# A routed stage two slots later and seven attention halves of nine slots, in a feed-forward / attention / feed-forward layer on one core

## The chip, the cores and the metric

The kernel runs on one core of one Trainium2 chip. The metric is the device time of one execution in microseconds (us); lower is better. TensorE is called PE below, VectorE DVE, ScalarE ACT, GpSimd POOL and SyncE SP, as in the profile.

## What is computed

The input `x` is four images of 512 x 512 f32 (2048 rows of 512). Three sublayers follow each other, each on a layer norm of its input:

```python
x = x + 0.5 * _L0_ffn_ref(_layernorm(x), w12, w3, router_w, expert_bias, sw1, sw2, sw3)
x = x + _L0_attn_ref(_layernorm(x), qkv_w, conv..., proj..., ln...)
x = x + 0.5 * _L0_ffn_ref(_layernorm(x), ...)          # the same weights again
```

`_L0_ffn_ref` adds a shared part, `silu(x @ sw1.T) * (x @ sw2.T) @ sw3.T` with 2048 hidden units, and a routed part: each row picks 2 of 8 experts (256 hidden units each) by a sigmoid router, and the experts' results are added with normalised weights. `_L0_attn_ref` is attention in windows of 8 tokens of 16 channels, with a three-tap convolution of the values, a projection and a norm.

## The kernel before, in words

**Slots.** The order of the work is written out by hand in slots, and all engines walk through the same slots. There are `SLOTS_ALL` = 128, in eight units of `UNIT` = 16: units 0 to 3 are the four images of the first feed-forward sublayer, units 4 to 7 those of the second. A slot `s` is 128 hidden units of the shared part for one image. PE does in it the gate product (12 matmuls, L1484), the up product (12, L1484), and the down product of the slot before it (12, L1498) into four PSUM banks. ACT makes the silu of the gate (L1694), DVE multiplies it with the up product (`sgh`, L1854), ACT takes the high bf16 half (L1704) and POOL the low half (L1812). The gate product of slot s+1 waits for the silu of s, the up product of s+1 for DVE's `sgh` of s, and the down product of s for POOL's low half. So DVE or ACT work that is late in a slot reaches PE in the next.

**Between the products** PE does small pieces into two side banks, listed with a slot and a position 0 to 5 in `PIECES` (L978 and on): the transposes and router logits of a row tile (`third`, `logits`; L463, L481), the transposes and products of attention (`turn` L1103, `qkv` L1120, `back`, `proj`, `out` L1301), and the lists of the routing (L749). ACT copies each piece out of its bank, in the order of its program, at the same position.

**Routed stages.** `ROUTED_AT` (L86) names the two slots ahead of which a routed stage of NB = 39 blocks stands, (23, 116): PE's L1607, L1620, L1632, rows gathered by POOL (L1801), results stored by SP in `sorted_y` (L1448). In the slots after it a class `Combine` adds the experts' results to the rows: `COMBINE_SLOT` (L1024 to 1026) gives tile m its slot. POOL gathers its two sets of rows from `sorted_y` (L665) and SP loads the row itself (L671, from `x2p`) one slot ahead; DVE adds (L686, L689); SP stores (L677). Three tiles are in flight: a buffer is free when the tile three before it has been stored. Tiles 28 to 31, the last image's, are not stored but stay in SBUF; tile 31's gather and load wait until tile 29 has been added. After slot 127 the down product of slot 127 is done, DVE adds the PSUM banks to tiles 28 to 31 (L578, `Evac(LAST).vec_sum`), and SP stores the output (L605).

**Evacuations.** `EVACS` (L523) gives ten slots (`EV_AT`) in which DVE adds an image's shared sum to rows that SP has loaded in slot `EV_LOAD` (L530 to 532). One of them stands at each routed stage (`EV_AT[1]`, `EV_AT[8]`), and the last at slot 128.

**Attention** is done for half an image at a time (8 halves), beside the slots. `D_SLOT` (L943) is where half h starts on DVE, `B_SLOT` where it ends (the next half's start). Slots `D_SLOT - 2` and `D_SLOT - 1` hold its `turn` and `qkv` pieces. DVE's 21 tasks of a half (products L1147, sums L1153, maxima, merging) are spread over the slots from `D_SLOT` to `B_SLOT` by `spare` and `WORK_SLOT`, a planner with fixed costs for each slot's other DVE work. `EXP_SLOT` is the slot after a maximum: ACT does the exponential there (L1203), at the end of its slot, with a table load before it and another before the next silu. `NORM_SLOT` is `B_SLOT + 2` (norm of the half, square root on ACT L1282), and `OUT_AT` two slots later. For image i the row tiles of the second feed-forward sublayer (`TILE`) begin when its second half is out, and the last image's tiles lead to the router, the lists (`LIST_SLOT`), and the gathers of the routed stage (`GATHER_SLOT`).

The slots of before:

| | before |
|---|---|
| `ROUTED_AT` | 23, 116 |
| `D_SLOT` | 29, 38, 47, 55, 64, 73, 81, 90 (the last half ends at 99) |
| slots of each half | 9, 9, 8, 9, 9, 8, 9, 9 |
| second `EXP_SLOT` of each half | 34, 43, 52, 61, 69, 78, 86, 95 |
| `turn` pieces of halves 1 to 7 | 36, 45, 53, 62, 71, 79, 88 |
| `LIST_SLOT[1]`, `GATHER_SLOT[1]` | 111, 114 |
| combine tiles 27 to 31 | 123, 124, 124, 125, 126 |
| shared weights reloaded (ACT queue; gate and up L304, 1 MB; down L311, 0.5 MB) | L304 in odd slots, the last in 123; L311 two slots after each |

Of the kernel before, what the change touches and what calls it, by code (L numbers as in the profile page):

```python
# [58 lines left out]
def macaron(nc, x, wall, rwT, ebias, qkvw, projw, projb, convw, convb, lnw, lnb, out):  # L59
# [7 lines left out]
    NT = ROWS // P  # L67
# [9 lines left out]
    HALVES = 2 * IMAGES  # L77
# [5 lines left out]
    UNIT = NU * KT  # L83
    UNITS = 2 * IMAGES
    SLOTS_ALL = UNITS * UNIT
    ROUTED_AT = (UNIT + 7, 7 * UNIT + 4)  # L86
    assert W3OFF + KT * D == WW and NB == 39 and UNIT == 16 and NU == E and NT == 16


# [12 lines left out]
    with ctx:  # L102
# [415 lines left out]
        def pool_root(e, q, var, root, n):  # L518
# [4 lines left out]

        EVACS = [(UNIT, 0, x, x1p, False), (ROUTED_AT[0], 1, x, x1p, False), (2 * UNIT, 1, x1p, x1d, True),
                 (3 * UNIT, 2, x1p, x1d, True), (4 * UNIT, 3, x1p, x1d, True), (5 * UNIT, 0, x2d, x2p, False),
                 (6 * UNIT, 1, x2d, x2p, False), (7 * UNIT, 2, x2d, x2p, False), (ROUTED_AT[1], 3, x2d, x2p, False),
                 (8 * UNIT, 3, None, out, False)]
        EV_AT = [ev[0] for ev in EVACS]
        EV_STORED = [16 * (v + 1 + sum(ev[4] for ev in EVACS[:v + 1])) for v in range(len(EVACS))]
        EV_LOAD = [at - 5 for at in EV_AT]  # L530
        EV_LOAD[0], EV_LOAD[1], EV_LOAD[2], EV_LOAD[3], EV_LOAD[4], EV_LOAD[5], EV_LOAD[6], EV_LOAD[8] = (
            UNIT - 2, EV_AT[1] - 4, EV_AT[2] - 2, EV_AT[3] - 3, EV_AT[4] - 4, EV_AT[5] - 3, EV_AT[6] - 2, EV_AT[8] - 1)
        LAST = len(EVACS) - 1

        class Evac:
# [404 lines left out]
        BIAS_SLOT, BIAS_STEPS = UNIT - 4, (4, 4, 4, 3)  # L940
        CONST_SLOT = 1
        LOADED, STATS, NORMED, HIGH, LOW, TURNED, LOGITS = range(7)
        D_SLOT = [ROUTED_AT[0] + 6 + 9 * h - h // 3 for h in range(HALVES)]  # L943
        LOAD_SLOT = [ROUTED_AT[0] + 1, ROUTED_AT[0] + 5] + [d - 4 for d in D_SLOT[2:]]
        B_SLOT = D_SLOT[1:] + [D_SLOT[-1] + 9]
        NORM_SLOT = [b + 2 for b in B_SLOT[:-1]] + [B_SLOT[-1] + 2]
# [28 lines left out]
        GATHER_SLOT = [s + 3 for s in LIST_SLOT]  # L975
        assert all(GATHER_SLOT[f] < ROUTED_AT[f] for f in range(2))

# [5 lines left out]
        for h in range(HALVES):  # L983
            d, b, end = D_SLOT[h], B_SLOT[h], h == HALVES - 1
            PIECES += [(d - 2, m, "turn", h, m) for m in range(2)]
# [29 lines left out]
        def spare(h, s):  # L1015

            left = 7.5 - 0.8 + sum(PE_SHARE.get(p[2], 1.0) for p in PIECES if p[0] == s)
            left -= sum(2.2 * (t[STATS] == s) + 0.6 * (t[NORMED] == s) + 0.7 * (t[HIGH] == s) + 0.7 * (t[LOW] == s) for t in TILE)
            left -= 7.0 * (s in NORM_SLOT) + 2.8 * (s in EV_AT)
            left -= sum(2.1 * (0 <= s - at - 1 < 2) + 0.3 * (0 <= s - at - 2 < 2) for at, ev in zip(EV_AT, EVACS) if ev[4])  # L1020
            left -= sum((1.5 + 2.0 * (m < TI)) * (at == s) for m, at in enumerate(COMBINE_SLOT))
            return max(left, 0.5)

        COMBINE_SLOT = [ROUTED_AT[0] + 1 + 2 * (m // 3) + m % 3 // 2 for m in range(8)]  # L1024
        COMBINE_SLOT += [2 * UNIT + 5 + m for m in range(8)]
        COMBINE_SLOT += [ROUTED_AT[1] + 2 * (m // 3) + m % 3 // 2 for m in range(NT)]
        WORK_SLOT = []
        for h, (d, b) in enumerate(zip(D_SLOT, B_SLOT)):
            left = [spare(h, s) for s in range(d, b)]
# [994 lines left out]
```

## Time and profile before

| | |
|---|---|
| three timed runs | 1465.43, 1465.55, 1476.45 us; median 1465.55 |
| the profiled execution | 1469.57 us |
| its span, first to last instruction | 1467.8 us |
| mean granted PE clock | 0.998 of full speed |
| PE busy | 1417.9 us, 97% |
| DVE, ACT, POOL busy | 952.1, 551.7, 502.1 us |

The span is what the rows below are times of, in us from its start; 1.77 us of the profiled execution lie around it. PE is busy nearly always, so what can be won or lost is in the places where it is not.

### The profile page before, as it was taken

The numbers are of one execution on the slowest core, as the hardware profiler recorded it, in microseconds if no ns is written. First come the engines' busy times: TensorE is split into PE (matmuls) and PEld (weight loads), VectorE is DVE, ScalarE is ACT, GpSimd is POOL, SyncE is SP. The second block draws the span as 40 slices with busy tenths as digits, with TensorE's granted clock in tenths as the row PEclk, the third lists the DMA queues.
The fourth block names the chain that finished last, engine by engine and source line by source line (L and its number), as shares of the span: only waits on it lengthen the run. The fifth ranks groups of instructions, "written<-read, shape, count | busy, mean of one in ns | idle before, by whom it ended". The sixth has DMA issues, their size and how long they took to land.

```text
span 1467.8 us, 22015 instructions
## 1 busy us (share of the span) xinstructions
PE 1417.9 (97%) x7642; PEld 679.6 (46%) x7642; DVE 952.1 (65%) x1295; ACT 551.7 (38%) x1153; POOL 502.1 (34%) x424
## 2 busy tenths in 40 slices
PE   4999999999989999999999999999999999999998
PEld 2444444444444444444444544445454444444443
DVE  5778853333348798998889889988935643333343
ACT  4566323333232433354544454345332213333211
POOL 2321132221244556263436343443512122221343
PEclk9999999999999999999999999999999999999999
DMA  9999668888493467174616562365327368898595
GB/s 305 306 351 320 267 143 206 194 196 183 165 279 119 153 189 235 44 215 132 185 52 181 168 144 83 112 188 143 109 87 227 103 183 219 188 195 185 189 300 185
DMA packets 233725, 272.63 MB, mean 186 GB/s; under 512 B 132243, under 2 KB 156819, under 8 KB 230163
## 3 DMA queue, kind: packets, MB, share of 16 engines
q1 hardware_dynamic: 198594, 166.34, 39.5%
q10 hardware_dynamic: 23664, 67.66, 14.7%
q0 software_dynamic: 11360, 37.23, 9.4%
q8 instruction: 66, 1.08, 0.3%
q14 instruction: 41, 0.33, 0.1%
HBM read 168.39 MB, written 72.88 MB: 164 GB/s over the span
## 4 chain that ended last, share of the span: by engine, by line
PE 62%; DVE 13%; issue 7%; DMA 3%; ACT 2%; POOL 2%; SPq 0%; POOLq 0%; ACTq 0%; DVEq 0%
PE bank L1484 25%; PE bank L1607 13%; PE bank L1498 12%; PE bank L1632 7%; DVE region L1147 3%; PE side L1120 1%; DVE region L1153 1%; DMA rows<-sorted_y,slots 1%; DVE sgh L1854 1%; PE side L1620 1%; POOL rows L665 1%; DVE rows L455 1%; PE side L1253 1%; DVE rows L446 1%; DMA region<-region 1%
## 5 line engine op out<-in xcount | busy, mean ns | idle before, releaser
L1484 PE MATMUL bank<-xT,wb 128*128 128x512 bf16 x2688 | 615.7, 381 | 23.6 <-DMA xT<-region 17.7
L1484 PEld LDWEIGHTS bank<-xT,wb 128*128 128x128 bf16 x2688 | 257.7, 98 | 324.9 <-issue 29.7
L1812 POOL TENSOR_TENSOR hs<-sgh,hs 128x512 bf16<-128x512 f32 x126 | 161.1, 1278 | 626.6 <-ACT hs L1704 626.5
L1498 PE MATMUL bank<-wb,hs 128*128 128x512 bf16 x1536 | 357.1, 379 | 0.2 <-POOL hs L1812 0.2
L1498 PEld LDWEIGHTS bank<-wb,hs 128*128 128x128 bf16 x1536 | 147.6, 98 | 173.3 <-issue 2.1
L1607 PE MATMUL bank<-wr,region 128*128 x912 | 221.7, 379 | 0.0
L1704 ACT ACTIVATE hs<-sgh 128x512 bf16<-128x512 f32 x128 | 81.4, 636 | 338.9 <-DVE sgh L1854 328.5
L1147 DVE TENSOR_TENSOR region<-region 128x1024 f32<-128x1024 f32 x128 | 186.9, 1482 | 1.1
L1854 DVE TENSOR_TENSOR sgh<-bank,sgh 128x512 f32<-128x512 f32 x128 | 88.0, 687 | 145.1 <-PE bank L1484 144.8
L1801 POOL DMA_INDIRECT region<-xnd,idxs x78 | 74.2, 952 | 221.3 <-DMA region<-region 214.0
L1694 ACT ACTIVATE sgh<-bank 128x512 f32<-128x512 f32 x128 | 76.6, 598 | 189.4 <-PE bank L1484 183.6
L1153 DVE TENSOR_REDUCE region<-region 128x256 f32<-128x2048 f32 x64 | 146.3, 2286 | 2.2
L1607 PEld LDWEIGHTS bank<-wr,region 128*128 128x128 bf16 x912 | 85.9, 98 | 89.9 <-issue 1.0
L1632 PE MATMUL bank<-wr,region 128*128 x468 | 113.7, 379 | 0.0
L1951 DVE TENSOR_TENSOR region<-bank,region 128x256 f32<-128x256 f32 x76 | 32.3, 425 | 97.8 <-ACT region L1742 91.3
L665 POOL DMA_INDIRECT rows<-sorted_y,slots x64 | 67.1, 1049 | 79.1 <-issue 73.7
L1742 ACT ACTIVATE region<-bank 128x256 f32<-128x256 f32 x76 | 29.2, 384 | 172.3 <-PE bank L1607 167.8
L1961 DVE COPY region<-side 128x512 bf16<-128x512 bf16 x78 | 33.1, 425 | 83.5 <-PE side L1620 83.5
L1484 PE MATMUL bank<-region,wb 128*128 128x512 bf16 x384 | 85.9, 379 | 1.5 <-DVE sgh L1854 1.5
L686 DVE SCALAR_TENSOR_TENSOR rows<-rows,coef 128x512 f32<-128x512 f32 x32 | 28.2, 880 | 71.6 <-DMA rows<-x2p 22.1
L1632 PEld LDWEIGHTS bank<-wr,region 128*128 128x128 bf16 x468 | 45.8, 98 | 55.2
L1484 PEld LDWEIGHTS bank<-region,wb 128*128 128x128 bf16 x384 | 37.4, 98 | 46.9 <-DVE sgh L1854 2.0
(182 smaller groups left out, 1356.0 us busy)
## 6 DMA issues: line engine op xcount, KB each, us to landing
wb<-wsplit ACTq DMA_DIRECT2D x42, 1024.0 KB
wb<-wsplit ACTq DMA_DIRECT2D x42, 512.0 KB
sorted_y<-region SPq DMA_DIRECT2D x78, 256.0 KB
wsplit<-wb SPq DMA_DIRECT2D x8, 1536.0 KB, 7.6
wr<-wall SPq DMA_DIRECT2D x6, 1536.0 KB, 9.8
rows<-x SPq DMA_DIRECT2D x32, 256.0 KB, 5.3
region<-xln SPq DMA_DIRECT2D x128, 64.0 KB, 2.6
xnd<-rows SPq DMA_DIRECT2D x30, 256.0 KB, 4.5
```

The lines of the kernel that those rows point to most:

```text
L665: e.indirect_dma_start(out=dst, out_offset=None, in_=sorted_y, in_offset=bass.IndirectOffsetOnAxis(ap=slots[:, self.f, k, self.t:self.t + ...
L1147: o.do(e.tensor_tensor(t, few.to_broadcast(full), many.to_broadcast(full), ALU.mult))
L1153: o.do(e.tensor_reduce(dst[:, (k - 1) * P:(k + 1) * P], self.tmp.rearrange("p (n c) -> p n c", c=H), AX.X, ALU.add))
L1484: m = e.matmul(ps[:], wb[:, w % 2, wp, at:at + P], xt[:, xp, c, :], start=(i == 0), stop=(i == 3 * NDC - 1))
L1498: m = e.matmul(psD[tt][:], hs[:, s % 2, hp, tt * P:(tt + 1) * P], wb[:, w % 2, wp, at:at + D], start=(first and i == 0), stop=(last and i ...
L1607: m = e.matmul(psH_of(k)[:], xsT[k % RX][:, xp * D + c * P:xp * D + (c + 1) * P], words_of(k, wp, c * D), start=(n == 0), stop=(n == 3 * N ...
L1632: m = e.matmul(psY[k % 2][:], hT[k % 2][:, hp, kt, :], words_of(k, wp, at), start=(n == 0), stop=(n == 3 * KT - 1))
L1694: e.activation(sgh[:, s % 2, :], psG[:], ACT.Silu).then_inc(S("h_silu").sem, 1)
L1704: e.activation(hs[:, s % 2, 0, :], sgh[:, s % 2, :], ACT.Copy).then_inc(S("h_hi").sem, 1)
L1801: e.indirect_dma_start(out=xs[k % RX], out_offset=None, in_=xnd, in_offset=bass.IndirectOffsetOnAxis(ap=idxs[:, k:k + 1], axis=0)).then_in ...
L1812: e.tensor_tensor(hs[:, s % 2, 1, :], sgh[:, s % 2, :], hs[:, s % 2, 0, :], ALU.subtract).then_inc(S("h_lo").sem, 1)
L1854: e.tensor_tensor(sgh[:, s % 2, :], psU[:], sgh[:, s % 2, :], ALU.mult).then_inc(S("h_mul").sem, 1)
```

## The change

The second routed stage stands ahead of slot 118 instead of 116 (its combine tiles move with it, and the last of them are held at slot 127), and the attention halves start one slot later from half 3 on, except half 5. Three loads of evacuations start one or two slots later.

```diff
-    ROUTED_AT = (UNIT + 7, 7 * UNIT + 4)
+    ROUTED_AT = (UNIT + 7, 7 * UNIT + 6)
...
         EV_LOAD = [at - 5 for at in EV_AT]
-        EV_LOAD[0], EV_LOAD[1], EV_LOAD[2], EV_LOAD[3], EV_LOAD[4], EV_LOAD[5], EV_LOAD[6], EV_LOAD[8] = (
-            UNIT - 2, EV_AT[1] - 4, EV_AT[2] - 2, EV_AT[3] - 3, EV_AT[4] - 4, EV_AT[5] - 3, EV_AT[6] - 2, EV_AT[8] - 1)
+        EV_LOAD[0], EV_LOAD[1], EV_LOAD[2], EV_LOAD[3], EV_LOAD[4], EV_LOAD[5], EV_LOAD[6], EV_LOAD[7], EV_LOAD[8] = (
+            UNIT - 2, EV_AT[1] - 4, EV_AT[2] - 2, EV_AT[3] - 3, EV_AT[4] - 4, EV_AT[5] - 2, EV_AT[6] - 1, EV_AT[7] - 3,
+            EV_AT[8] - 1)
...
-        D_SLOT = [ROUTED_AT[0] + 6 + 9 * h - h // 3 for h in range(HALVES)]
+        D_SLOT = [ROUTED_AT[0] + 6 + 9 * h - (h > 4) for h in range(HALVES)]
...
-        COMBINE_SLOT += [ROUTED_AT[1] + 2 * (m // 3) + m % 3 // 2 for m in range(NT)]
+        COMBINE_SLOT += [min(ROUTED_AT[1] + 2 * (m // 3) + m % 3 // 2, SLOTS_ALL - 1) for m in range(NT)]
```

What these give, worked out from the formulas:

| | after |
|---|---|
| `ROUTED_AT` | 23, 118 |
| `D_SLOT` | 29, 38, 47, 56, 65, 73, 82, 91 (the last half ends at 100) |
| slots of each half | 9, 9, 9, 9, 8, 9, 9, 9 |
| second `EXP_SLOT` of each half | 34, 43, 52, 61, 70, 79, 87, 96 |
| `turn` pieces of halves 1 to 7 | 36, 45, 54, 63, 71, 80, 89 |
| `LIST_SLOT[1]`, `GATHER_SLOT[1]` | 112, 115 |
| combine tiles 27 to 31 | 125, 126, 126, 127, 127 |
| `EV_LOAD` of the evacuations at 80, 96, 112 | 78, 95, 109 (before: 77, 94, 107) |

## Rows read from the trace of the kernel before

**Rows 1.** The page: busy time of the engines.
```profile
PE 1417.9 (97%) x7642; PEld 679.6 (46%) x7642; DVE 952.1 (65%) x1295; ACT 551.7 (38%) x1153; POOL 502.1 (34%) x424
```

**Rows 2.** Timeline of PE, slots 51 to 95: start, length, instruction, [idle before it, releaser].
```profile
631.36 1.47 PE L1484 MATMUL bank<-xT,wb 128*128 128x512 bf16 x6 [1.62 <-ACT sgh L1694]
...
698.55 0.20 PE L481 MATMUL side<-rw,xT 128*128 128x24 bf16 x2 [0.72 <-ACT rows L472]
...
737.15 0.92 PE L1120 MATMUL side<-wqkv,region 64*128 64x192 f32 x8 [1.12 <-ACT region L1112]
...
861.00 0.20 PE L481 MATMUL side<-rw,xT 128*128 128x24 bf16 x2 [0.33 <-ACT rows L472]
...
870.89 0.66 PE L1301 MATMUL side<-ident,region 128*128 128x128 f32 x4 [0.46 <-ACT region L1306]
...
893.67 0.92 PE L1120 MATMUL side<-wqkv,region 64*128 64x192 f32 x8 [2.60 <-ACT region L1112]
...
1026.39 0.66 PE L1301 MATMUL side<-ident,region 128*128 128x128 f32 x4 [0.18 <-ACT region L1306]
```

**Rows 3.** Timeline of PE, the later places where it sat idle over 0.5 us.
```profile
1136.80 0.38 PE L463 MATMUL side<-identb,rows 128*128 128x128 bf16 x4 [1.48 <-DVE rows L455]
...
1188.52 0.75 PE L749 MATMUL side<-rows 128*128 128x78 bf16 x16 [0.60 <-DVE rows L743]
...
1386.05 2.76 PE L1484 MATMUL bank<-region,wb 128*128 128x512 bf16 x12 [1.48 <-DVE sgh L1854]
```

**Rows 4.** Timeline of ACT at the end of slot 78: half 5's second exponential.
```profile
888.81 1.28 ACT L1203 ACT_TABLE_LOAD   x1
890.11 0.63 ACT L1203 ACTIVATE region<-region 128x512 f32<-128x512 f32 x1
...
891.24 1.28 ACT L1694 ACT_TABLE_LOAD   x1
```

**Rows 5.** Timeline of PE and DVE at the end of slot 48's up product.
```profile
611.43 2.76 PE L1498 MATMUL bank<-wb,hs 128*128 128x512 bf16 x12
...
612.07 0.68 DVE L1854 TENSOR_TENSOR sgh<-bank,sgh 128x512 f32<-128x512 f32 x1
```

**Rows 6.** Busy times by stretch, slots 27 and 28; granted clock after the five engines.
```profile
413.00:421.00 8.00, 6.23 (x19) 3.35 (x20) 3.35 (x7) 1.79 (x3) 2.51 (x3) 0.57 0.79 239
```

**Rows 7.** Timeline of PE, slots 126 and 127: the down products that follow the up product.
```profile
1450.81 2.75 PE L1498 MATMUL bank<-wb,hs 128*128 128x512 bf16 x12
...
1458.58 2.75 PE L1498 MATMUL bank<-wb,hs 128*128 128x512 bf16 x12
```

**Rows 8.** Timeline of SP, its queue: the loads of the combine tiles 27 and 28 on.
```profile
1430.19 0.47 SPq L671 DMA_DIRECT2D rows<-x2p  x1
...
1439.32 6.88 SPq L671 DMA_DIRECT2D rows<-x2p  x4
```

**Rows 9.** Timeline of DVE, slots 123 to the end: combine tiles 27, 28, 31, and the last sums.
```profile
1437.38 0.75 DVE L686 SCALAR_TENSOR_TENSOR rows<-rows,coef 128x512 f32<-128x512 f32 x1 [6.99 <-DMA rows<-x2p]
...
1442.83 0.75 DVE L686 SCALAR_TENSOR_TENSOR rows<-rows,coef 128x512 f32<-128x512 f32 x1 [3.31 <-DMA rows<-x2p]
...
1445.78 0.68 DVE L1854 TENSOR_TENSOR sgh<-bank,sgh 128x512 f32<-128x512 f32 x1
...
1453.57 0.75 DVE L686 SCALAR_TENSOR_TENSOR rows<-rows,coef 128x512 f32<-128x512 f32 x1 [1.79 <-DMA rows<-sorted_y,slots]
...
1462.43 2.63 DVE L578 SCALAR_TENSOR_TENSOR rows<-bank,rows 128x512 f32<-128x512 f32 x4 [2.89 <-PE bank L1498]
```

**Rows 10.** Timeline of POOL: tile 31's second gather, and slot 127's low half.
```profile
1450.04 0.95 POOL L665 DMA_INDIRECT rows<-sorted_y,slots  x1 [0.31 <-issue]
...
1460.28 1.15 POOL L1812 TENSOR_TENSOR hs<-sgh,hs 128x512 bf16<-128x512 f32 x1 [6.61 <-ACT hs L1704]
```

**Rows 11.** Timeline of ACT: a reload of shared weights (its queue), and slot 127's high half.
```profile
1430.43 0.53 ACTq L304 DMA_DIRECT2D wb<-wsplit  x1
...
1459.58 0.63 ACT L1704 ACTIVATE hs<-sgh 128x512 bf16<-128x512 f32 x1 [2.73 <-DVE sgh L1854]
```

## The prediction

> **What bounds the kernel now.** I read the page first, then the list of PE's waits, then PE's timeline for every idle place, and last the timelines of DVE, ACT, POOL and SP around those places. PE is busy 1417.9 us of 1467.8 [rows 1]; no other engine is above 65%. So the time is PE's work, which the change leaves alone (the same products, pieces and blocks in another order), and about 50 us in which PE sits idle. Of these, some 39 us lie before slot 51 or behind the last product and are not moved by the change of slots; in the reach of the change are seven places in the attention stretch, 1.62 + 0.72 + 1.12 + 0.33 + 0.46 + 2.60 + 0.18 = 7.03 us [rows 2], and three later ones, 1.48 + 0.60 + 1.48 = 3.56 us [rows 3]. If all ten went, the gain would be 10.6 us, 0.7%. That is the ceiling, and it is below 1% (14.7 us), which is about what a measurement of this kernel can tell from no change.
>
> **The routed stage two slots later.** It removes and adds no instruction. Its 39 blocks follow each other on PE without a gap in the trace, and a gap of 1.48 us comes behind it, where DVE waited in the stage's first slot for the first gathered rows and was then late for the up product (the row at 1386.05) [rows 3]. The tiles, their gathers and loads, and the even and odd slots of the weight reload move by two together, so this gap moves along: 0, bounded by its whole loss (-1.48) and by as much again (+1.48). Ahead of the stage the gathers get a slot more of slack; nothing waited there, so that is worth 0. The last image's tiles, routing and lists come one slot later. The 1.48 at L463 (DVE busy with two tiles in one slot) moves with them. The 0.60 at L749 stays too: DVE has one list and the evacuation together in slot 112, before and after; only it is now the first list. 0 for both, with bounds of -2.1 and +1.5 (one more such wait).
>
> **The end.** Here the change costs. Tile 31's place would be slot 128 and is cut to 127, and tiles 28 to 31 now stand in slots 126, 126, 127, 127. I call U the end of the last up product, 1458.58, and a slot without pieces is 1458.58 - 1450.81 = 7.77 us [rows 7]. Everything of tiles 27 to 30 comes two slots (15.54 us) later against U: what stood at a time t of the trace stands at t - 1443.04 from U.
> - Tile 27's load was issued at 1430.19 and used at 1437.38, 7.2 us later; a reload of shared weights, 1 MB, was issued beside it at 1430.43 [rows 8, 9, 11]. The last reload from an odd slot leaves at 123, so in its new place, slot 124 to 125, none is beside it. Tile 28's load, which had none either, took 1442.83 - 1439.32 = 3.5 us [rows 8, 9]. I take 3.5 us: issued at U - 12.85, used at -9.35, two DVE additions of 0.79 us each: done at -7.75.
> - Then SP stores 27 and loads 28 and 29, at -7.4; used at -3.9; both tiles take 1445.78 - 1442.83 = 2.95 us [rows 9]: done at -0.95, so DVE's `sgh` of slot 127 is not held up.
> - Tile 31's two gathers wait for that. POOL does them in its slot 126, ahead of the low half of slot 127: 0.95 + 0.30 + 0.95 = 2.2 us [rows 10], until +1.25. The low half can only start when the high half is there, 1460.21 - 1458.58 = +1.63 [rows 10, 11]; so the last down product is not delayed.
> - The rows land 1453.57 - 1450.99 = 2.6 us after the gather's issue ends [rows 9, 10], at +3.85. Tile 31's row load, issued at about -0.95, is there by +2.6. Meanwhile DVE does `sgh` and tile 30. Tile 31: two additions, 1.6 us, to +5.4. The four last sums, 2.63 us [rows 9], to +8.1. Before they ended at 1465.06 - 1458.58 = +6.5.
> So the end is 1.6 us later. Bounds: if the gathers land before DVE asks for them, DVE has `sgh`, then tiles 30 and 31 (3.2 us) behind it: 0.95 + 3.2 + 2.63 = +6.8, or 0.3 later. If tile 27's load takes 7.2 us in its new place too, all of it is 3.7 us later: the gathers stand until +4.95, the low half until +6.1 (before +2.85, 1460.28 + 1.15), so PE waits 3.25 us, and the last sum ends at +11.8: 5.3 later. I take 1.6, since the loads in question are nearest to the row without a reload beside them.
>
> **The halves.** The exponential of a half ends its ACT slot; with two table loads it keeps ACT for 1.28 + 0.63 + 1.28 us, and the copy of the next half's `turn` piece stands behind the first two of these [rows 4]. This costs PE where the second exponential is in the slot right before the `turn`: before, at slots 52/53, 61/62, 78/79. PE waited 0, 1.12 and 2.60 us for it [rows 2]. After, there are two such pairs, 70/71 and 79/80. Half 4 (8 slots from 65) has the planner's task list of half 2 before it (8 slots from 47) to within a task: 0. Half 5 (9 slots from 73) has that of half 3 before it (9 slots from 55) to within a task: 1.12. So 3.72 becomes 1.12: 2.60 gained.
> The 1.62 us in slot 51 come from a late silu: in slot 49 to 50 DVE was late with the norm of half 1 and ACT's root behind it. Half 2 had four products and two sums in slot 47; now it has three products and one sum, and slot 48 costs the same as before. DVE was 612.07 - 611.43 = 0.64 us late at the end of slot 48 [rows 5], and that lateness goes: 0.6 gained, 1.0 stays. The other four (1.69 us together) are copies of tiles' and halves' pieces that are short of time by under a microsecond; their slots shift against each other and I let them stand at 0 change. Sum of the halves: -3.2 us, with bounds of -7.0 (all gone) and +1.0: if both new pairs cost what the worst old one did, 5.2 us stand for 3.72 (+1.5), less the 0.6. Where such a wait goes, DVE's `sgh` of that slot is late next; PE needs it only after a down and a gate product, 2 x 2.59 us, so a lateness like the 2 to 3 us that goes with it stays hidden.
> One rule of the Trainium skill would make this larger: "ScalarE: Activation LUTs", section "What ACT_TABLE_LOAD costs", says that a switch of tables costs the load and a drain of 1380 ns behind it, 2.66 us in all. By this each pair would hold ACT for over 5 us and the pair removed would be worth about twice as much. The trace shows no drain: the load from 888.81 takes 1.28 us and the exponential begins 0.02 us behind it [rows 4].
>
> **The loads of evacuations.** Those of slots 80, 96 and 112 are issued one or two slots later, for they wait for tiles that come later. The tightest is that of 96, issued in slot 95 behind the piece at position 4. Four loads take under 7.2 us to land in the worst row for such a load [rows 8, 9], and their sums must be done when the down product of slot 96 begins, a whole slot after its up product; at 7.77 us a slot they fit, by about 1 us in that worst case. Worth 0; if the cover were gone, 1 to 2 us.
>
> **Sum.** -3.2 + 1.6 + 0 = -1.6 us. The profiled execution was 1469.57 us (1467.8 and 1.77 around), so a profile of after would be 1468.0. The median of the runs is 4.02 us below the profiled execution; a part may be that in slots 27 and 28 the granted clock was 0.57 over 8 us [rows 6], which is 3.4 us lost to the lower of the two levels, 1.2 GHz, after PE had sat idle for a load. Nothing before slot 47 is changed, so I leave this difference as it is: 1465.55 - 1.6 = 1464.0 us.
>
> **Rivals.**
> - **A: the combine queue runs into slot 127 (slower).** Tile 27's load does not get faster, tile 31's gathers hold POOL ahead of the last low half, PE waits and the last sums come late: +5.3, with the halves' -3.2 it is +2.1, 1467.7 us; up to 1470.8 if the halves give nothing. It decides from where the load takes 1.6 us longer than 3.5, that is 5.1 us, for then the end costs the 3.2 that the halves give. For it: DVE waited 6.99 and 3.31 us for such loads [rows 9]. Against it: the reload beside it is gone. Chance 0.25.
> - **B: nine slots are enough everywhere.** All seven waits of rows 2 go: -7.0 + 1.6 = -5.4, 1460.1 us. For it: all come from late ACT or DVE. Against it: two exponentials still stand right before a `turn`. Chance 0.15.
> - **C: the waits only move.** The shifted slots meet evacuations and tiles in new ways, and the halves give 0: +1.6, 1467.2 us. For it: six of the seven waits are under 1.7 us, each a chance meeting. Chance 0.18.
> - **D: the clock.** PE sits idle in a new place and is granted 1.2 GHz for a while: 3.4 us for each stretch as in rows 6. Four or more would be needed to pass 1%. Chance 0.04, here for slower by over 1%.
> - **The forecast**, 0.38, with an own range of 1462 to 1466.
>
> **The range.** The low end is case B with half a microsecond less, 1459.5; the high end case A with the halves giving almost nothing, 1470.5. Faster by over 1% lies beyond the ceiling of 10.6 us and would need something that I don't see: 0.01. Slower by over 1%: case D, 0.04. Within 1%: 0.95.
>
> **What would show it.** Right: in PE's timeline of the two waits for L1112 (1.12 and 2.60 us) one is left, of about 1 us, in slot 80, and there is none in slots 54, 63 and 71; the wait of 1.62 us in slot 51 is near 1.0; the routed stage is followed by a wait of about 1.5 us; tile 27's row is used 3 to 4 us after its load; DVE's last four sums end about 8 us after the last up product. Wrong: a PE wait for POOL (L1812) of several us before the last down product (case A); no waits over 0.5 us between slots 51 and 104 (case B); several new ones there that add to 7 us (case C); a clock under 0.99 in the mean (case D).

## The result and the profile after

The changed kernel is slower: 1473.4 us median (1471.16 to 1476.34, 5 runs) against 1465.82 us (1465.43 to 1476.45, 5 runs); the ratio of the runs is 1.0039, 95% interval 1.0021 to 1.0057, that is +5.7 us (+3.1 to +8.4). The profiled execution of after is 1472.36 us, with a span of 1470.6. The forecast was 1464.0 with a range up to 1470.5; the outcome lies beyond it, on rival A's side.

The two profiles differ by only 2.8 us in their spans, because they differ already where nothing was changed. DVE's product of slot 46, the last slot before half 2's new plan, starts at 594.37 us before and at 589.98 after (some waits were shorter, and PE ran at the lower clock for 3.4 us there, from 83.3 us on, instead of the 6.8 us of [rows 6]). So I count from there. The busy times by stretch have the lengths: slots 46 to 99 (the halves), 99 to 115, 115 to the end of the last up product (routed stage, combine tiles), and from there to the last instruction. Before:

```profile
594.37:1069.12 474.75, 467.23 (x2604) 230.05 (x2603) 431.36 (x435) 214.09 (x495) 206.28 (x139) 1.00 0.47 136
1069.12:1203.62 134.50, 132.42 (x728) 63.42 (x727) 65.23 (x141) 36.94 (x65) 27.20 (x24) 1.00 0.47 144
1203.62:1458.58 254.96, 253.48 (x1291) 119.25 (x1289) 85.68 (x166) 69.12 (x141) 78.17 (x79) 1.00 0.79 216
1458.58:1467.80 9.22, 5.51 (x25) 2.17 (x23) 3.32 (x5) 0.63 (x1) 1.15 (x1) 1.00 0.31 114
```

After (stretch, its length, busy PE, weight load, DVE, ACT, POOL; granted clock):

```profile
589.98:1062.97 472.99, 464.10 (x2560) 230.77 (x2611) 424.84 (x430) 215.71 (x496) 203.32 (x139) 1.00 0.47 137
1062.97:1197.77 134.80, 131.72 (x713) 63.28 (x727) 70.71 (x146) 37.05 (x65) 27.73 (x24) 1.00 0.43 132
1197.77:1455.29 257.52, 253.79 (x1266) 119.75 (x1289) 78.32 (x159) 69.13 (x141) 76.74 (x77) 0.99 0.83 215
1455.29:1470.60 15.31, 7.10 (x24) 2.53 (x23) 8.79 (x13) 0.63 (x1) 3.45 (x3) 0.84 0.40 137
```

The halves gave 1.76 us, slots 99 to 115 took 0.3, the third stretch 2.56, the end 6.09: together +7.2 us, in the timed interval. The places, in PE's timeline after:

```profile
627.94 1.47 PE L1485 MATMUL bank<-xT,wb 128*128 128x512 bf16 x6 [2.32 <-ACT sgh L1695]
...
807.22 0.63 PE L1104 MATMUL side<-ident,region 128*128 128x128 f32 x4 [1.00 <-DMA region<-xln]
...
895.29 0.92 PE L1121 MATMUL side<-wqkv,region 64*128 64x192 f32 x8 [1.11 <-ACT region L1113]
...
1182.08 0.75 PE L750 MATMUL side<-rows 128*128 128x78 bf16 x16 [0.60 <-DVE rows L744]
...
1396.61 4.45 PE L1485 MATMUL bank<-region,wb 128*128 128x512 bf16 x12 [2.41 <-DVE sgh L1855]
...
1462.34 4.40 PE L1499 MATMUL bank<-wb,hs 128*128 128x512 bf16 x11 [4.30 <-POOL hs L1813]
```

Of the seven waits of [rows 2] the two for the `turn` copy have become one of 1.11 us, as forecast; the one in slot 51 has grown from 1.62 to 2.32; one of 1.00 for a half's load is new. The 1.48 behind the routed stage is 2.41, and before the last down product stands a wait of 4.30 us for POOL, which was 0.16 before. After both long waits PE runs its matmuls at the lower of its two clock levels (1.2 GHz) for a while; in the first line the four microseconds after the wait, in the second those after the 4.30 us:

```profile
1397.00:1401.00 4.00, 4.00 (x13) 1.47 (x11) 0.96 (x2) 0.81 (x2) 3.25 (x3) 0.57 0.86 256
1462.00:1466.00 4.00, 3.61 (x9) 1.33 (x11) 2.20 (x4) 0.00 (x0) 0.28 (x1) 0.57 0.18 56
```

At 0.57 over 4 us, 1.7 us of full speed are lost to PE each time. The first loss is in the third stretch: 0.93 us more wait and these 1.7 us make its 2.56. The second costs the kernel nothing in this profile. DVE begins the last sums when tile 31 is added (1465.22) and does the four without a pause, so PE, slow or not, is ahead of them. The five runs of after have mean clocks of 0.994 to 0.997. The profile of before has 0.998, but before's runs beside e5 to e12 go from 0.994 to 1.000, so these means alone tell little.

The end itself is in DVE's, POOL's and SP's timelines after. DVE:

```profile
1447.00 0.75 DVE L687 SCALAR_TENSOR_TENSOR rows<-rows,coef 128x512 f32<-128x512 f32 x1 [5.13 <-DMA rows<-x2p]
...
1455.25 0.75 DVE L687 SCALAR_TENSOR_TENSOR rows<-rows,coef 128x512 f32<-128x512 f32 x1 [6.11 <-DMA rows<-x2p]
...
1458.15 0.68 DVE L1855 TENSOR_TENSOR sgh<-bank,sgh 128x512 f32<-128x512 f32 x1
...
1463.77 0.75 DVE L687 SCALAR_TENSOR_TENSOR rows<-rows,coef 128x512 f32<-128x512 f32 x1 [3.48 <-DMA rows<-sorted_y,slots]
1464.56 0.75 DVE L690 SCALAR_TENSOR_TENSOR rows<-rows,coef 128x512 f32<-128x512 f32 x1
1465.22 2.48 DVE L579 SCALAR_TENSOR_TENSOR rows<-bank,rows 128x512 f32<-128x512 f32 x4
```

The row loads in the timeline of SP's queue, after:

```profile
1441.67 0.49 SPq L672 DMA_DIRECT2D rows<-x2p  x1
...
1448.94 9.64 SPq L672 DMA_DIRECT2D rows<-x2p  x4
```

POOL's timeline of after:

```profile
1448.15 1.21 POOL L666 DMA_INDIRECT rows<-sorted_y,slots  x1 [0.30 <-issue]
...
1458.51 0.95 POOL L666 DMA_INDIRECT rows<-sorted_y,slots  x1 [4.77 <-DVE rows L690]
1459.76 1.34 POOL L666 DMA_INDIRECT rows<-sorted_y,slots  x1 [0.30 <-issue]
1461.12 1.16 POOL L1813 TENSOR_TENSOR hs<-sgh,hs 128x512 bf16<-128x512 f32 x1
```

Tile 27's row was used 5.3 us after its load (1441.67 to 1447.00), tile 28's 6.3 us after (1448.94 to 1455.25), where I had 3.5 for both. In the first of them nearly all was moved after 3.3 us; the busy times by stretch show the DMA engines almost still behind that, at 8 GB/s (the last number; before it their busy share):

```profile
1441.67:1445.00 3.33, 3.33 (x17) 1.54 (x16) 0.20 (x1) 0.63 (x1) 1.76 (x2) 1.00 0.85 300
1445.00:1446.00 1.00, 1.00 (x6) 0.42 (x5) 0.00 (x0) 0.60 (x1) 0.69 (x2) 1.00 0.05 8
```

Tiles 28 and 29 then hold DVE's product of slot 127 until 1458.15, 2.9 us behind the up product (1455.29); tile 31's gathers wait for tile 29's sum and stand ahead of the low half of slot 127, which ends at 1462.3. The last sums end 12.4 us behind the last up product, against 6.5 before.

### The profile page after: what moved, and what is told of

The parts are those of the page before. It is cut to its first block, busy times and chain, and to the rows that moved or that the text cites. A ratio compares the mean times of both kernels' runs of the same rounds, so it can differ in the third digit from the quotient of the medians.

```text
span 1470.6 us, 21867 instructions
## 1 busy us (share of the span) xinstructions
PE 1410.4 (96%) x7493; PEld 679.7 (46%) x7642; DVE 946.5 (64%) x1295; ACT 553.7 (38%) x1154; POOL 499.2 (34%) x424
## 4 chain that ended last, share of the span: by engine, by line
PE 62%; DVE 10%; issue 6%; DMA 6%; ACT 2%; SPq 1%; POOL 1%; POOLq 0%; DVEq 0%; ACTq 0%
PE bank L1485 24%; PE bank L1608 13%; PE bank L1499 12%; PE bank L1633 7%; DMA rows<-x2p 2%; DMA rows<-sorted_y,slots 2%; PE side L1121 2%; DVE region L1148 1%; PE side L1621 1%; DMA region<-xln 1%; DVE rows L687 1%; DVE rows L690 1%; PE side L1254 1%; POOL rows L666 1%; DVE sgh L1855 1%
## 5 line engine op out<-in xcount | busy, mean ns | idle before, releaser
L1485 PE MATMUL bank<-xT,wb 128*128 128x512 bf16 x2613 | 605.7, 381 | 27.3 <-DMA xT<-region 17.8
L1608 PE MATMUL bank<-wr,region 128*128 x889 | 216.8, 379 | 1.2
L1633 PE MATMUL bank<-wr,region 128*128 x458 | 111.6, 379 | 0.5
L687 DVE SCALAR_TENSOR_TENSOR rows<-rows,coef 128x512 f32<-128x512 f32 x32 | 25.1, 784 | 73.6 <-DMA rows<-x2p 31.1
```

The lines of the kernel that those rows point to most:

```text
L1485: m = e.matmul(ps[:], wb[:, w % 2, wp, at:at + P], xt[:, xp, c, :], start=(i == 0), stop=(i == 3 * NDC - 1))
L1608: m = e.matmul(psH_of(k)[:], xsT[k % RX][:, xp * D + c * P:xp * D + (c + 1) * P], words_of(k, wp, c * D), start=(n == 0), stop=(n == 3 * N ...
L1633: m = e.matmul(psY[k % 2][:], hT[k % 2][:, hp, kt, :], words_of(k, wp, at), start=(n == 0), stop=(n == 3 * KT - 1))
```

## Experiments

Each kernel was timed against the kernel before on the same chip. "End" is from the last up product to the last instruction, "halves" from slot 46 to 99, each in that kernel's profile (before: 9.2 and 474.75 us). Waits are PE's, in us. Ratios of after, of e1 to e4, of e5 to e8, of e9 to e11 and of e12 come from five separate comparisons, and the profile is one execution of each.

| | ratio to before, 95% | halves | wait in slot 51 | behind the routed stage | PE's wait for POOL at the end | end |
|---|---|---|---|---|---|---|
| before | 1 | 474.75 | 1.62 | 1.48 | 0.16 | 9.2 |
| after | 1.0039 (1.0021-1.0057) | 472.99 | 2.32 | 2.41 | 4.30 | 15.3 |
| e1 | 1.0048 (1.0030-1.0067) | 474.81 | 2.32 | 1.87 | under 0.3 | 9.2 |
| e2 | 1.0038 (1.0023-1.0052) | 474.55 | 1.62 | 1.73 | 3.02 | 13.7 |
| e3 | 1.0016 (1.0003-1.0028) | 474.31 | 2.32 | 1.76 | 2.11 | 13.2 |
| e4 | 1.0046 (1.0033-1.0059) | 472.68 | 2.32 | 1.43 | 2.56 | 17.3 |
| e5 | 1.0004 (0.9993-1.0015) | 474.86 | 2.32 | 2.04 | 2.15 | 13.4 |
| e6 | 1.0023 (1.0011-1.0035) | 472.62 | 2.32 | 3.20 | 1.72 | 12.7 |
| e7 | 1.0010 (0.9996-1.0024) | 474.05 | 2.33 | none | 1.31 | 12.1 |
| e8 | 0.9999 (0.9979-1.0019) | 474.70 | 1.62 | none | under 0.3 | 9.5 |
| e9 | 0.9999 (0.9985-1.0013) | 473.28 | 2.32 | 1.56 | 0.72 | 10.7 |
| e10 | 0.9997 (0.9980-1.0014) | 476.49 | 2.31 | 0.68 | 0.72 | 10.0 |
| e11 | 0.9981 (0.9967-0.9994) | 472.78 | 1.50 | none | 1.50 | 11.8 |
| e12 | 0.9996 (0.9979-1.0013) | 473.66 | 1.46 | 1.74 | 1.50 | 11.9 |

**e1: the halves alone.** 
```diff
-    ROUTED_AT = (UNIT + 7, 7 * UNIT + 6)
+    ROUTED_AT = (UNIT + 7, 7 * UNIT + 4)
```


> The change without its first part: the second routed stage stays ahead of slot 116, the attention halves and evacuation loads are those of after. Theory 'the end' (the loss is made by combine tiles 28 to 31 in slots 126 and 127: late product on DVE, POOL's low half behind tile 31's gathers, PE idle before the last down product): the loss is gone, 1 to 4 us faster than before (1462 to 1465), and DVE's last sums end about 6.5 us behind the last up product as before. Theory 'the halves' (their new slots cost in the timed runs, by waits or by a lower clock after them): still 3 to 8 us slower than before.

The end is that of before (9.2 us), but the kernel is 7.0 us slower, where 1 to 4 us faster was expected if only the end made the loss. PE's waits in this profile show what the later halves do when the routed stage does not move:

```profile
1205.22 2.76 PE L1608 MATMUL side<-wr,region 128*128 x12 [1.67 <-DMA region<-region]
...
1212.50 1.47 PE L1608 MATMUL bank<-wr,region 128*128 x6 [1.93 <-DMA region<-region]
```

The gathers for the stage are issued in slot 115, one slot ahead of it, and its first blocks wait 1.67 + 1.93 = 3.6 us for their rows. With 118 no first block waits (in e4 a later one does once, 1.06 us): the two slots of delay pay for the halves' slot. From slot 46 on this profile takes 5.0 us more than before's, of which these are 3.6. And the gain of the halves is lost to the clock: the wait in slot 51 is 2.32 us as in after, and here the clock falls behind it (granted clock 0.57 in the column before the last two), where in after it did not:

```profile
626.00:630.00 4.00, 1.68 (x9) 0.60 (x8) 3.93 (x4) 3.37 (x4) 2.60 (x2) 1.00 0.00 0
630.00:634.00 4.00, 4.00 (x15) 2.01 (x14) 3.83 (x11) 3.13 (x4) 2.83 (x3) 0.57 0.34 130
```

That brings the halves' stretch back to 474.8 us. In the nine profiles with a wait of about 2.3 us there, the length of this stretch falls in two groups: 472.6 to 473.3 (after, e4, e6, e9), and 474.0 and more (e1, e3, e5, e7, e10): the second group are those with the lower clock behind the wait. So the 1.8 us that the halves give are lost again in five of these nine executions.

**e2: the routed stage alone.** 
```diff
-        D_SLOT = [ROUTED_AT[0] + 6 + 9 * h - (h > 4) for h in range(HALVES)]
+        D_SLOT = [ROUTED_AT[0] + 6 + 9 * h - h // 3 for h in range(HALVES)]
```
(and `EV_LOAD` as before)

> The first part alone: routed stage ahead of slot 118 with its combine tiles, halves and loads as before. Theory 'the end': the whole loss and none of the small gain, 6 to 9 us slower than before; PE idle about 4 us for POOL before the last down product, last sums ending about 12 us behind the last up product. Theory 'the halves': within 2 us of before.

5.6 us slower (3.4 to 7.6), a little less than the 6 to 9 expected; the end is 4.5 us longer than before's (6.1 in after) and PE waits 3.02 us for POOL. The last sums end 10.8 us behind the up product (1457.81 to 1468.64). The first part of the change makes the end long with no help from the halves.

**e3: tile 31 on buffers of its own.** 
```diff
                 if m == 2 * NT - 1:
-                    self.r = T(6)
+                    self.a, self.b, self.r = (words(R_QKV + k * D, D) for k in range(3))
...
-                    e.wait_ge(S("c_sum").sem, 2 * NT - 2)
+                    return
```


> After, with three buffers of its own for combine tile 31 (in the region that the routed stage has left free) and semaphores of its own, so that its gathers and its load wait for no other tile. Theory 'the end': POOL is free for slot 127's low half, so PE's wait of 4.3 us shrinks to the 2 to 3 us by which DVE's product of slot 127 is late; last sums end 8 to 10 us behind the last up product; 2 to 4 us faster than after, about as before or up to 3 slower. If POOL's wait had no part in it: as after.

As expected: PE's wait falls to 2.11 us and the end by 2.1 us. The ratio is 1.0016 where it was 1.0039; the two intervals overlap. By the profile the wait of tile 31's gathers for tile 29 costs some 2 us.

**e4: tile 31's gathers behind the low half.** 
```diff
-                        if c.m % NT >= WAYS:
+                        if c.m % NT >= WAYS and c.m < 2 * NT - 1:
                             c.pool_gather(e)
+                    if s == SLOTS_ALL - 1:
+                        Combine(2 * NT - 1).pool_gather(e)
```


> After, with tile 31's two gathers behind the low half of slot 127 in POOL's order instead of ahead of it. Theory 'the end' in two parts: PE's wait before the last down product falls from 4.3 to about 3 us (what DVE's late product leaves), but the gathers start 2 us later, so tile 31's sum and with it the end come 1 to 3 us later than in after. If only POOL's order made the loss: 2 to 4 us faster than after.

PE's wait falls to 2.56 us, which is what DVE's late product leaves, and the end is 2.0 us longer than in after, as tile 31's sum starts at 1467.94, 10.5 us behind the up product. Both parts count: POOL's order for PE, the gathers' landing for the last sums. Swapping them only moves the loss; the timed runs (1.0046 against 1.0039) can't tell the two kernels apart.

**e5: own buffers for tiles 28 to 31, rows loaded early.** 
```diff
-                if m == 2 * NT - 1:
-                    self.r = T(6)
+                if m >= KEPT:
+                    self.a, self.b, self.r = (words(R_QKV + (3 * (m - KEPT) + k) * D, D) for k in range(3))
...
+                    if 4 <= s - ROUTED_AT[1] < 4 + TI:
+                        Combine(KEPT + s - ROUTED_AT[1] - 4).sp_load(e)
```


> After, with three buffers of their own for each of combine tiles 28 to 31 (twelve, in the region the routed stage has left free), their row loads issued in slots 122 to 125 ahead of SP's stores, and no waits for other tiles. Theory 'the end is a chain of buffers' (store, load, add, gather): the chain is cut, PE's wait for POOL before the last down product is under 0.5 us, the last sums end about 6.5 to 7.5 us behind the last up product instead of 12.4, and the kernel is 4 to 6 us faster than after, so within 2 us of before. Rival 'the DMA engines are full' (about 290 GB/s in the last slots whatever waits): the gathers still land late, PE waits 2 us or more, and it is at most 2 us faster than after.

The time came as expected (5 us below after, level with before), the profile only in part: PE still waits 2.15 us for POOL. POOL's timeline says why:

```profile
1454.24 1.15 POOL L1821 TENSOR_TENSOR hs<-sgh,hs 128x512 bf16<-128x512 f32 x1 [0.52 <-ACT hs L1713]
1455.54 1.24 POOL L668 DMA_INDIRECT region<-sorted_y,slots  x1
1457.08 1.39 POOL L668 DMA_INDIRECT region<-sorted_y,slots  x1 [0.30 <-issue]
1458.78 0.95 POOL L668 DMA_INDIRECT region<-sorted_y,slots  x1 [0.30 <-issue]
1460.03 0.95 POOL L668 DMA_INDIRECT region<-sorted_y,slots  x1 [0.30 <-issue]
1460.99 1.16 POOL L1821 TENSOR_TENSOR hs<-sgh,hs 128x512 bf16<-128x512 f32 x1
```

Nothing is waited for, but the four gathers of tiles 30 and 31 take 5.4 us of POOL between the low halves of slots 126 and 127, and they start late because tile 27's row (4.65 us of wait) made slot 126 late.

**e6: only the rows' loads early.** e5 with the gathers' buffers and waits as in after.

> As e5, but only the rows' own loads (from x2p) of tiles 28 to 31 have buffers of their own and leave early; the gathers stay where they are, and tile 31's still waits for tile 29's sum. If the row load behind the store is what makes DVE late at slot 127 (5.3 and 6.3 us of wait in after), DVE's product of slot 127 comes within 1 us of the last up product's end and PE's wait for POOL falls below 1.5 us: 3 to 5 us faster than after. If the gathers are as late as the loads, DVE waits for them instead, and the gain is under 2 us.

DVE's product of slot 127 now starts 0.6 us behind the up product (1460.77 and 1460.15), so the row loads behind the stores were what made it late; PE's wait is 1.72 us (under 1.5 was expected) and the end 12.7 us. The gain on after is 2.3 us by the ratios, less than the 3 to 5 expected; in this profile 3.20 us were lost behind the routed stage, with the clock at the lower level after it.

**e7: stage at 117, combine tiles one slot behind it, with the buffers of e5.** 
```diff
-    ROUTED_AT = (UNIT + 7, 7 * UNIT + 6)
+    ROUTED_AT = (UNIT + 7, 7 * UNIT + 5)
...
-        COMBINE_SLOT += [min(ROUTED_AT[1] + 2 * (m // 3) + m % 3 // 2, SLOTS_ALL - 1) for m in range(NT)]
+        COMBINE_SLOT += [min(ROUTED_AT[1] + 1 + 2 * (m // 3) + m % 3 // 2, SLOTS_ALL - 1) for m in range(NT)]
```


> The halves of after, the routed stage ahead of slot 117, the first combine tiles one slot behind it (118) instead of in its first slot, the last at 127, and the own buffers of e5. Expected: the first block is not waited for (a slot of slack, against 1.7 and 1.9 us in e1), no wait for DVE behind the routed stage (1.5 to 2.4 us before), the end as in e5; about 3 us faster than before in the stretches, less what the lower clock takes. If the wait behind the routed stage comes from something else than the combine tiles in its first slot, it stays.

The wait behind the stage is gone, so it does come from the combine tiles in its first slot. A new one of 2.59 us stands in the stage's first blocks, after DVE's evacuation had waited for its rows (L579, 1.09 and 1.05 us, from x2d); it is there again in e10 (2.69) and e11 (1.27, after 3.43 for a block's rows), all three with the stage ahead of an odd slot, and in none with 116 or 118. I read it as the evacuation's loads meeting the weight reload of the odd slot before; that was not tested. The 3 us of gain that were expected did not come: from slot 46 on this profile takes 5.3 us more than before's, and the timed runs are level with before.

**e8: before, with the later combine tiles and own buffers.** The same two edits on the kernel before.

> Before (old halves, routed stage ahead of 116) with its combine tiles one slot later (117 to 127) and the own buffers of e5. Expected: the 1.48 us wait behind the routed stage is gone, the end is no longer than before (9.2 us from the last up product to the last instruction): 1 to 3 us faster than before. If a tile in slot 127 costs by itself, whatever its buffers: 2 us or more slower.

The profile does what was expected (no wait, end 9.5 us, 1.4 us shorter from slot 46 on), and a tile in slot 127 costs nothing by itself. The 1 to 3 us of gain expected are not seen in the timed runs (1463.69 to 1479.26), which can't tell it from before.

**e9: e5 with the gathers spread.** 
```diff
+                    early = {SLOTS_ALL - 4: [KEPT], SLOTS_ALL - 3: [KEPT + 1, KEPT + 2], SLOTS_ALL - 2: [KEPT + 3]}
-                    for c in combines(s + 1):
+                    for c in [c for c in combines(s + 1) if c.m < KEPT] + [Combine(m) for m in early.get(s, [])]:
```


> e5 (own buffers for tiles 28 to 31) with POOL's eight gathers of them spread: tile 28 in slot 124, 29 and 30 in slot 125, 31 alone in slot 126, where e5 has two tiles in each of 125 and 126. Theory 'four gathers of 1.25 us each stand ahead of slot 127's low half': PE's wait for POOL, 2.15 us in e5, falls below 0.6 us and the end from the last up product on is about 10 to 11 us instead of 13.4: 1 to 3 us faster than e5, as fast as before or 1 to 2 us faster. If the wait is DVE's late product instead, it stays at 2.

POOL's timeline of e9:

```profile
1455.96 1.24 POOL L668 DMA_INDIRECT region<-sorted_y,slots  x1
1457.50 0.95 POOL L668 DMA_INDIRECT region<-sorted_y,slots  x1 [0.30 <-issue]
1458.88 1.71 POOL L1821 TENSOR_TENSOR hs<-sgh,hs 128x512 bf16<-128x512 f32 x1 [0.43 <-ACT hs L1713]
```

With two gathers ahead of it the low half waits for ACT again, PE waits 0.72 us (under 0.6 was expected), and the end is 10.7 us. In the profile this takes from slot 46 on 873.6 us, against 873.4 before and 880.6 after. In the timed runs it is level with before, and 0.5 thousandths from e5, less than can be told.

**e10 and e11: e7 with the gathers spread, and with half 2 at eight slots.** 
```diff
-        D_SLOT = [ROUTED_AT[0] + 6 + 9 * h - (h > 4) for h in range(HALVES)]
+        D_SLOT = [ROUTED_AT[0] + 6 + 9 * h - (h > 4 or h == 3) for h in range(HALVES)]
```
(the second edit, e11 only)

> e7 (halves of after, routed stage ahead of 117, first combine tiles one slot behind it, own buffers) with the gathers spread as in e9. Expected: no wait behind the routed stage, PE's wait for POOL at the end (1.3 us in e7) under 0.6 us, and 1 to 3 us faster than before in the timed runs if the 2.59 us wait inside the routed stage of e7 was a single event; if it comes back, 0 to 2 us slower.

> e10 with half 2 back at eight slots (47 to 54) and half 3 from 55 with ten. Theory 'half 2's ninth slot takes DVE work out of slot 47, which had time for it, and leaves slot 48 as full as it was': the wait of 2.32 us in slot 51 is 1.62 us again as in before, and no stretch of lower clock follows it. Rival: the wait comes from the norm of half 1 alone: it stays at 2.3.

e10 is level with before, its odd-slot wait back, and two of the waits expected to be small or absent are 0.68 us (behind the stage) and 0.72 us (for POOL). e11 has 1.50 us in slot 51, so half 2's ninth slot made the longer wait; no lower clock follows there, nor in e12 (1.46), before, e2 and e8 (1.62). e11 is the only kernel whose interval lies below 1 (0.9967 to 0.9994), by 2.8 us. Its profile doesn't show that gain: from slot 46 on it takes 881.0 us, as long as after's 880.6 and 7.5 us more than before's. Its span is short (1467.2 us) because slot 46 begins at 586.22 us, 8.2 us earlier than in before, and in the slots up to there the two kernels do the same. The timed gain goes with the clock: means of 0.997 to 0.999 in all twelve runs, 0.994 to 0.999 in before's 29. Why the clock was higher is not known.

**e12: e9 with half 2 at eight slots.**

> e9 (routed stage ahead of 118 as in after, own buffers, gathers spread) with half 2 at eight slots as in e11. Expected: the wait in slot 51 at 1.5 to 1.6 us instead of 2.32, PE's wait for POOL at the end under 1 us, no wait inside the routed stage (those of e7, e10 and e11 came with its odd slot 117), one of about 1.5 us behind it: 1 to 3 us faster than before in the timed runs, as e11. If e11 owes its time to the combine tiles' later first slot, this one is no faster than before.

The waits are as expected but for POOL's (1.50, where under 1 was expected), and the time is level with before (0.9979 to 1.0013), not 1 to 3 us faster. So e11's gain is not confirmed by its nearest relative, and of twelve comparisons one just beyond its interval is thin; I would call e11 no slower than before in the timed runs; a gain that comes from the changed slots is not shown.

## Why the prediction was wrong, step by step

- **What bounds the kernel**: held. PE's work is unchanged, and all differences are waits and the clock behind them. The ceiling of 10.6 us for a gain was not approached by any version. That the later loads of the evacuations cost nothing held too: in after PE waits nowhere over 0.3 us between slot 80 and the 1.49 us at L463.
- **The end**: this step failed. I took tile 27's and 28's row loads at 3.5 us because no weight reload is issued beside them, from one row of before [rows 8, 9]. They measured 5.3 and 6.3, so DVE's last product was late where I had it on time. The load of tile 28 is the larger part: it left 1.1 us later than I had it, took 2.8 us more, and together that is 3.9 us. In before, the tile 28 row that I copied had the gathers of tiles 28 and 29 ahead of it (tile 27 had been so late that they had been issued, 1432.95 to 1437.67, before the load at 1439.32 left); a 0.5 MB reload, which I had overlooked, was issued at 1440.73, but only 0.06 MB of it had moved when the row was used. In after the gathers are issued up to 1449.36 and the load leaves at 1448.94, in the middle of them. While DVE waited for it, the gathers' queue moved 0.78 MB in after and 0.19 MB in before; in e2, e3 and e4 it was 0.36 to 0.55 MB and the same load took 4.2 to 4.4 us. In all, 287 GB/s were moved in after and 295 in before, so the engines were as full both times; the queue of the row's load had 44% of their time in after and 67% in before. No weights were moved beside it in after. I read it so: what was beside the load was replaced, not removed; no run takes the gathers alone away.
  Tile 27's 5.3 us are another matter. The gathers of tiles 28 and 29 begin to move only at 1446.0, and the engines were almost still for a microsecond before that. The last of the queue's packets come one behind the other, as from one of the 16 engines, until 1446.5. In the same window one packet of 16 KB of another queue (q8, instruction) takes 0.95 us from 1444.42 on; such a packet lies in this load's window in e2, e3 and e4 too, where it took 5.5 to 5.9 us. Whether it holds the last packets up was not tested, so the cause of tile 27's time stays open.
  From there the chain ran as the step had it, and close to the figures of rival A: DVE 2.9 us late (A: 2.7), PE idle for POOL 4.30 (A: 3.25), last sums at +12.4 (A: +11.8), the end 6.1 us longer (A: 5.3). That A came so near is in part luck. It put the whole delay of 3.7 us on tile 27's load and left tile 28's at 3.5; measured, 2.8 of 3.9 us came from tile 28's. The end is bound by tile 31: its gathers are issued until 5.8 us behind the up product, its rows are added from +8.5 on, and the sums follow; the lower clock behind the wait of 4.30 is not in that chain. e2 shows that the routed stage alone makes 4.5 of the 6.1 us, e3, e4 and e5 that the gathers' wait and POOL's order have a part in it, e6 that the row loads make DVE late.
- **The halves**: right in sign, 1.76 us instead of 3.2. The pairs of exponential and `turn` came out to the digit (1.11 left of 3.72, 2.6 gained). Of the other four waits, 1.69 us together and forecast to stay, one of 0.71 is left that is over 0.3 us. The 0.6 us in slot 51 had the wrong sign, +0.70: the ninth slot took 3.4 us of DVE work out of slot 47, and DVE idled there (1.98 us before its product at 606.28, then 1.28 for PE before the evacuation), while slot 48 kept its load and its product beside POOL took 2.98 us (1.22 elsewhere). e11, with half 2 at eight slots, confirms that the ninth slot did it. Work taken from a slot ahead of a wait buys nothing behind it. And a new wait of 1.00 us came at a `turn` that waits for its half's load: in the 8-slot half 4 the load and the output of half 3 now fall in one slot (69). That can't be the whole cause: in before the same two fall together in slots 51 and 77, without such a wait.
- **The routed stage**: "this gap moves along" held in kind; its length varies from kernel to kernel (1.4 to 3.2 us), with its bound of twice 1.48 passed once, in e6. Its 2.41 us in after and the clock behind it cost 2.6 us that I had at 0. That nothing waits ahead of the stage held with 118; e1 shows that it would not with 116, where the later halves leave the gathers one slot.
- **Rival D, the clock**: I priced it only as a way beyond 1% and gave the forecast nothing for it. It should have been a possible term for each lengthened wait: 1.7 us behind the 2.41 in after, and 1.7 behind the 2.32 in five of nine profiles. Behind the 4.30 the clock fell too, but off the chain that ends last.
- **The chances**: within 1% held. A, at 0.25, was priced with the halves' full 3.2 us; with 1.8 it gives 1469.1, and with the 2.6 us behind the routed stage 1471.7; the ratio makes it 1471.5 (the median of the runs is 1473.4).

## What to carry to other kernels

A transfer's time read from a row belongs to what else was in flight then; before copying it to a new place, list the transfers issued within its length there and just ahead of it, the kernel's own gathers among them, and look at the same transfer in other slots for its spread (here 3.5 to 7.2 us). At the end of a kernel, count every engine's instructions between the last two steps that PE needs (here 1.25 us of POOL for each gather), since no later slot absorbs them. And spend slack only in front of the wait that it should shorten: check in which slot the planner takes the work away.

## What was not expected of the hardware

- Some waits of PE were followed by 3.4 us at the lower clock level, 1.7 us lost, and others of the same place were not (slot 51: with a wait of 2.3 us in five of nine profiles, with 1.5 to 1.6 us in none of five). The length of the wait doesn't settle it. In after the clock fell behind a wait of 1.93 us at 82.3; it did not fall behind the 2.60 us for the `turn` copy in before, e2 and e8, nor behind 2.69 us in e10. Which of the timed runs had it can't be seen; of after's five runs the mean clocks, 0.994 to 0.997, mean 4.4 to 8.8 us each.
- A load can be nearly done and still be waited for: behind tile 27's in after, 1445 to 1446, only 8 GB/s were moved.
- e1's timed runs (1471.53 to 1480.05) are further above before's than its profile explains (7.0 us, against 5.0 from slot 46 on). That stays open.
